# A quarter of layer 1's running sums moved from GpSimd to VectorE, and the head-masked tile stored the other way round

## What is computed

```python
ss = jax.nn.sigmoid(x @ Ws).reshape(b, t, H, E)      # H = 8 heads, E = 5 experts
sd = jax.nn.sigmoid(x @ Wd).reshape(b, t, H, E)
ms, md = _topk_mask(ss, K), _topk_mask(sd, K)        # K = 3
q = jnp.einsum('bthed,bthe->bhtd', q5, sd * md)      # q5, k5, v5: x @ W, five experts of 8 x 64
k = jnp.einsum('bthed,bthe->bhtd', k5, ss * ms)
v = jnp.einsum('bthed,bthe->bhtd', v5, ss * ms)
attn = jax.nn.softmax(jnp.einsum('bhid,bhjd->bhij', q * scale, k), axis=-1)
out = jnp.einsum('bhij,bhjd->bihd', attn, v)
o5 = jnp.einsum('bthd,dm->bthm', out, Wo)...
return jnp.einsum('bthem,bthe->btm', o5, md)
```

## Time and profile before

| | |
|---|---|
| time, median of 3 | 3302.1 us (3296.39 to 3312.5) |
| the profiled execution | 3312.5 us, span 3310.7 us |
| mean granted TensorE clock | 0.882 |
| busy in the span: TensorE, VectorE, ScalarE, GpSimd | 89%, 56%, 40%, 43% |
| products of layer 1 | 372 to 1293 us |

### The profile page before, as it was taken

One profiled execution on the slowest core, in us unless ns is written; L12 is line 12 of the kernel. 1 busy time (PEld: TensorE's weight loads), 2 busy tenths in 40 slices (PEclk: granted clock), 3 DMA queues, 4 the chain that ended last, 5 costly groups with the idle time before them and its releaser, 6 DMA issues.

```text
span 3310.7 us, 38793 instructions
## 1 busy us (share of the span) xinstructions
PE 2952.2 (89%) x13864; PEld 1823.9 (55%) x13864; DVE 1841.8 (56%) x3075; ACT 1314.4 (40%) x3221; POOL 1429.1 (43%) x1348
## 2 busy tenths in 40 slices
PE   7896799999999998799999999999789788888876
PEld 3564355555555555355555554444478666666765
DVE  6868577677777766465655554444433534343313
ACT  4453433443443343345555555444412342413201
POOL 3324366676676776267777775000013200101144
PEclk8997899999999999799999999998777775857666
DMA  5451100000000000600000000221022111111111
GB/s 183 151 181 53 50 1 1 1 1 1 1 1 1 1 1 1 145 17 14 1 1 1 1 1 20 74 74 64 30 64 87 43 28 37 31 40 39 34 39 45
DMA packets 160928, 128.88 MB, mean 39 GB/s; under 512 B 97688, under 2 KB 136864, under 8 KB 160224
## 3 DMA queue, kind: packets, MB, share of 16 engines
q1 hardware_dynamic: 148832, 90.13, 9.7%
q0 software_dynamic: 11904, 36.27, 3.4%
HBM read 105.70 MB, written 38.47 MB: 44 GB/s over the span
## 4 chain that ended last, share of the span: by engine, by line
PE 49%; DVE 4%; ACT 3%; issue 2%; another core or an unknown queue 1%; SPq 0%; POOL 0%; DMA 0%; DVEq 0%; ACTq 0%
PE bank L63 44%; PE bank L2051 4%; DVE work L3178 1%; DVE work L3180 1%; SPq L3198 0%; DVE work L3137 0%; ACT L3105 0%; PE bank L2749 0%; DVE weights_even L3137 0%; DVE work L1984 0%; DVE work L3294 0%; POOL weights_odd L2814 0%; PE bank L2904 0%; ACT work L3106 0%
## 5 line engine op out<-in xcount | busy, mean ns | idle before, releaser
L63 PE MATMUL bank<-work 64*128 64x256 f32 (+5 forms) x4384 | 654.3, 365 | 28.1 <-DVE work L3294 7.9
L1491 POOL TENSOR_TENSOR work<-work 128x512 f32<-128x512 f32 x384 | 494.9, 1289 | 320.4 <-DVE work L1483 303.4
L63 PEld LDWEIGHTS bank<-work 64*128 64x128 f32 (+4 forms) x4384 | 468.3, 185 | 260.2 <-issue 137.3
L2039 POOL TENSOR_SCALAR work<-work 128x256 f32<-128x256 f32 x512 | 465.0, 926 | 240.9 <-DVE work L2030 240.8
L63 PE MATMUL bank<-weights_odd,normed_channels 128*128 128x512 f32 (+3 forms) x1152 | 527.9, 566 | 22.4 <-DVE work L1483 15.4
L63 PE MATMUL bank<-work,weights_even 128*32 128x128 f32 (+4 forms) x1136 | 344.9, 482 | 50.0 <-DVE work L1010 15.7
L2024 ACT ACTIVATE work<-bank,work 128x256 f32<-128x256 f32 x512 | 235.9, 473 | 195.0 <-DVE work L2010 190.9
L1483 DVE TENSOR_TENSOR work<-bank,work 128x512 f32<-128x512 f32 x360 | 245.5, 686 | 110.0 <-PE bank L63 106.5
L63 PEld LDWEIGHTS bank<-weights_odd,normed_channels 128*128 128x128 f32 x1152 | 186.6, 199 | 161.5 <-issue 83.1
L63 PEld LDWEIGHTS bank<-work,weights_even 128*32 128x32 f32 (+4 forms) x1136 | 162.2, 193 | 194.4 <-issue 136.4
L2783 POOL TENSOR_TENSOR weights_odd<-weights_odd 128x512 f32<-128x512 f32 x40 | 50.7, 1267 | 491.6 <-ACT weights_odd L2778 491.6
(11 more groups left out here) (307 smaller groups left out, 4535.4 us busy)
## 6 DMA issues: line engine op xcount, KB each, us to landing
work<-gate_rows_L SPq DMA_DIRECT2D x64, 256.0 KB, 3.1
filter_matrices<-in_L_filters SPq DMA_DIRECT2D x24, 512.0 KB, 8.1
work<-filter_matrices SPq DMA_DIRECT2D x16, 768.0 KB, 4.2
expert_rows_in<-in_zeros SPq DMA_DIRECT2D x8, 640.0 KB, 11.3
weights_odd<-expert_rows_in SPq DMA_DIRECT2D x40, 128.0 KB
expert_rows_out<-weights_odd SPq DMA_DIRECT2D x40, 128.0 KB
weights_even<-expert_rows_in SPq DMA_DIRECT2D x20, 128.0 KB
expert_rows_out<-weights_even SPq DMA_DIRECT2D x20, 128.0 KB
```

What stands on the lines that cost most here:

```text
L63: return pe.matmul(out, lhsT, rhs, start=first, stop=last, skip_group_check=True)
L1491: gp.tensor_tensor(self.sum_of(p), self.sum_of(p), self.product_of(p), ALU.add).then_inc(s["l1_add"], 1)
L2039: gp.tensor_scalar(p[:, c], p[:, c], self.sums(n, half, i), None, ALU.mult).then_inc(s["l2_p"], 1)
```

## The change

The second add of every sum (e = 2) is done on VectorE, in its list two slots behind the product (`vector_add`, right after that slot's `vector_product`); GpSimd keeps e = 1, 3 and 4. The semaphore `l1_add` now counts VectorE's adds, one a sum, and a new one, `l1_add_pool`, GpSimd's three; all waits on the old count are rewritten. GpSimd's add for e = 3 waits for VectorE's, VectorE's waits for GpSimd's e = 1. The tile `kept` holds the heads one after the other, 64 words each: GpSimd writes in order, and VectorE's reduce reads at a step of 64 words.

```diff
     def wait_product_free(self, on, p):
-        on.wait_ge(self.k.sem["l1_add"], p // 5 * 4 + p % 5 - 3)
+        n = p // 5 * 4 + p % 5 - 1 - 3
+        if n >= 0:
+            total, e = n // 4, n % 4 + 1
+            if e == 2:
+                on.wait_ge(self.k.sem["l1_add"], total + 1)
+            else:
+                on.wait_ge(self.k.sem["l1_add_pool"], 3 * total + {1: 1, 3: 2, 4: 3}[e])
...
+    def vector_add(self, v, on, p):
+        if p % 5 == 2:
+            s, total = self.k.sem, p // 5
+            on.wait_ge(s["l1_add_pool"], 3 * total + 1)
+            on.wait_ge(s["l1_prod"], p + 1)
+            v.tensor_tensor(self.sum_of(p), self.sum_of(p), self.product_of(p), ALU.add).then_inc(s["l1_add"], 1)
+
     def gpsimd_add(self, gp, on, p):
         s, total, e = self.k.sem, p // 5, p % 5
-        if e > 0:
+        if e in (1, 3, 4):
             on.wait_ge(s["l1_prod"], p + 1)
-            on.wait_ge(s["l1_add"], 4 * total + e - 1)
-            gp.tensor_tensor(self.sum_of(p), self.sum_of(p), self.product_of(p), ALU.add).then_inc(s["l1_add"], 1)
+            if e == 3:
+                on.wait_ge(s["l1_add"], total + 1)
+            if e == 4:
+                on.wait_ge(s["l1_add_pool"], 3 * total + 2)
+            gp.tensor_tensor(self.sum_of(p), self.sum_of(p), self.product_of(p), ALU.add).then_inc(s["l1_add_pool"], 1)
...
     def tensor_turn(self, pe, on, p):
-        on.wait_ge(s["l1_add"], 4 * (p // 5) + 4)
+        on.wait_ge(s["l1_add_pool"], 3 * (p // 5) + 3)
...
     def tensor_times_v(self, pe, on, n):
-        on.wait_ge(s["l1_add"], 4 * (6 * bt + 5) + 4)
+        on.wait_ge(s["l1_add_pool"], 3 * (6 * bt + 5) + 3)
...
     def gpsimd_kept(self, gp, on, n):
-        gp.tensor_tensor(self.kept[n % 2].rearrange("p (d h) -> p h d", h=L1_H), heads(self.o[i]), self.per_head(self.mask[g % 3], tile, 1, e),
+        gp.tensor_tensor(heads(self.kept[n % 2]), heads(self.o[i]), self.per_head(self.mask[g % 3], tile, 1, e),
                          ALU.mult).then_inc(s["l1_kept"], 1)
...
     def vector_over_heads(self, v, on, n):
         v.tensor_reduce(self.heads_mixed[m % 2][:, e * L1_DH:(e + 1) * L1_DH],
-                        self.kept[n % 2].rearrange("p (d h) -> p d h", h=L1_H), AX.X, ALU.add).then_inc(s["l1_over"], 1)
+                        self.kept[n % 2].rearrange("p (h d) -> p d h", d=L1_DH), AX.X, ALU.add).then_inc(s["l1_over"], 1)
...
             if slot < L1_UNITS * BATCH:
                 self.vector_product(v, on, slot)
+            if 0 <= slot - 2 < L1_UNITS * BATCH:
+                self.vector_add(v, on, slot - 2)
```

More of the change, by code:

```diff
@@ L1240, in __init__ @@
                   "l1_scan", "l1_c", "l1_mixed", "l1_merge_mm", "l1_merged", "l1_route_mm", "l1_scored", "l1_picks", "l1_prod_mm", "l1_prod",
-                  "l1_add", "l1_turn_mm", "l1_turned", "l1_score_mm", "l1_max", "l1_exp", "l1_pt_mm",
[1 row of a table added]
                   "l1_pt", "l1_pt_act", "l1_pv", "l1_inverse", "l1_o", "l1_kept", "l1_over", "l1_comb_turn", "l1_at",
```

## The result

The changed kernel took 3339.1 us (median of seven, 3331.1 to 3356.4) against 3311.8 us of the kernel before, run beside it: ratio 1.0096, 95% interval 1.0066 to 1.0126. By the ratio that is 32 us slower, by the two medians 27, where +34 was forecast. The profiled execution has a span of 3337.0 us.

The account below looks back on a forecast made before the run. VectorE, not TensorE, was taken to set the pace in layer 1's full routing stretch. The terms +20, +8, +10, -5 and +1 made +34 us, so 3336 us against the 3302.1 us median, range 3290 to 3376.

Parts of the forecast that it names:

- The bound: Layer 1's routing stretch, 896 to 936 us: VectorE, busy 37.1 of 40 us, sets the pace, not TensorE.
- Term 1: Full routing stretch, seven times: added adds and slower reduces on VectorE, less idle time and standing still, +20 us.
- Terms 2 and 3: VectorE's catching up at 837 to 847, eight times, +8 us; later products elsewhere in layer 1, +10 us.
- Term 5: Tail behind the last product: reduces follow GpSimd's multiplies one by one, +1 us.
- Term 4: TensorE's 15.0 us wait for late sums: a third comes back, -5 us.
- relief decides: Rival: cheap reduce and TensorE's whole wait for sums gone make the kernel faster, 3279 us; chance 0.09.
- the terms' ends: Lower and upper sizes of the terms, giving the likeliest case's own range, stated as 3314 to 3358 us.
- The reduce: VectorE's head reduce, reading single words 64 words apart: 1.11 us instead of 0.676, +0.435 us each.
- The rival with a full read rate: Head reduce reads at full rate, so no change, 3297 us; chance 0.23 shared with everything hidden.
- The added adds: VectorE's 96 new adds: 0.61 us of queue each, not 1.31, because GpSimd is kept idle then.
- The buffer wait: At `vector_add`: the new wait for GpSimd costs nothing, since the product ahead of it already waited.

Follow-up runs that it names:

- GpSimd's relief alone: Kernel before with GpSimd's second add of each sum left out and done by nobody, old layout: ratio 1.0009, products' stretch 916.9 us.
- the pair add: Kernel before, but VectorE adds product e = 2 into e = 3's buffer and GpSimd adds the pair: ratio 1.0041, products' stretch 934.9 us.
- the additional adds: Kernel before plus 96 VectorE adds of two SBUF inputs that nothing waits for, each right behind product e = 3: ratio 1.0040.

## Why the prediction was right

**The bound.** Right: VectorE in the routing stretch, not TensorE's 94% nor GpSimd's load. 29 of the 32 us lie there, and spreading the routing takes 16.5 us off the changed kernel where it takes 4.5 off the one before. What the experiments do not bear out is that VectorE's added time alone sets the price: equal time in adds and in reduces cost 14 and 6 us.

**Term 1, the full stretch, +20 us forecast.** Right in mechanism and low in size: 4.2 us a group, 29 us. The work added was less than assumed, 4.9 us for 6.7: 4 adds and 7 reduces at +0.36 in the routing's own length. But of the 2.9 us idle that the sum used up, only 1.3 were used, and the -1.0 for less standing still did not come. The six routing lines went from 87.8 to 89.5 us in all. Of their excess over 0.48 us, what they stood behind GpSimd's adds fell from 23.5 to 13.4 us, as the term had it, and what they stood behind its multiplies into `kept` rose from 10.4 to 22.2: the steps met other instructions.

**Terms 2 and 3, catching up and elsewhere, +18 us.** Too high. The rest of a group grew by 0.3 us, eight times 2 to 3 us. Elsewhere VectorE has slack, and it seems that TensorE makes up for a product that is a little late; no run isolates this. **Term 5, the tail, +1 us**, is right: 51.7 us from the last product to the end of layer 1, for 50.6.

**Term 4, late sums, -5 us.** Wrong. The row was misread: ScalarE's copy ended the wait. GpSimd's relief alone was worth 3 us in the stretch, and the growth of that wait to 37 us cost nothing that the pair add gives back. The rival "relief decides" rested on the same row and falls with it. Terms 1 and 4 were too low by 9 and 5 us, terms 2 and 3 too high by 16; that the total, +34, is so near to +32 is partly luck. So is 3336 beside 3339: it stands on the 3302.1 of three executions, and beside the changed kernel the old one took 3311.8. A slip in the sum changed nothing: the terms' ends as they are stated give 3310 to 3362, and not 3314 to 3358.

**The reduce.** 1.11 us taken from the nearest row, 1.03 measured, +0.357 for +0.435. The range that the Trainium skill's stream rates gave (Vector Engine (DVE) Microarchitecture Reference, "Measured stream behaviour on trn2"), 0.96 to 1.36 us, holds the measurement. The rival with a full read rate is out.

**The added adds.** 0.61 of queue each as taken, for a reason only half right. GpSimd was idle then, as argued; but the additional adds show that an instruction right behind the product would have kept its time even with GpSimd on its way. By the Trainium skill (GPSIMD Engine Reference, "Key points") two SBUF inputs contend with GpSimd. The trace agrees, 1.19 for 0.48, and the order decides which engine pays.

**The buffer wait.** Right: no wait of `vector_add` for GpSimd is in the trace.

## What to carry to other kernels

Cut a mean load up by stage before moving work: an engine at 73% on average can be full in a third of the time, and most of the price of what it is given is paid in that third. The price is not proportional: the two edits cost 14 and 6 us alone and 32 together. Nor is it the same for equal time: adds cost more than twice what reduces did, so measure the instruction that you mean to move. Before counting on a wait in a table, look at the timeline for the event that ended just before the waiter started.

## What was not expected of the hardware

Of a GpSimd add and a VectorE instruction with two SBUF inputs, the second in time is held, and 0.16 us are enough to decide: VectorE's add of two SBUF inputs right behind the product kept its 0.48 us and GpSimd's add took 1.45 us for 1.27, while a step that came 0.43 us behind GpSimd's start took 1.19 for 0.48. A reduce of 512 elements that reads single words 64 words apart takes 1.03 us, for 0.68 when it reads them in order, and GpSimd's multiply that writes in order instead of at a step of 8 words takes 1.06 for 1.13.
